# Gate attention of a decoder kernel: causal mask of the transposed scores by an elementwise minimum on VectorE

## What is computed

```python
x = _rmsnorm(hidden_states, ln1_w)
# _attention(x, Wq, Wk, Wv, Wo):
q = (x @ Wq.T).reshape(b, s, H, HD)
k = (x @ Wk.T).reshape(b, s, H, HD)
v = (x @ Wv.T).reshape(b, s, H, HD)
scores = jnp.einsum('bqhd,bkhd->bhqk', q, k) / np.sqrt(HD).astype(np.float32)
causal = jnp.tril(jnp.ones((s, s), bool))
scores = jnp.where(causal, scores, jnp.finfo(scores.dtype).min)
probs = jax.nn.softmax(scores, axis=-1)
out = jnp.einsum('bhqk,bkhd->bqhd', probs, v).reshape(b, s, d)
attn = out @ Wo.T
mod = MOD_SCALE * jnp.tanh(attn @ A)
```

## Time and profile before

| | us |
|---|---|
| median of 3 runs | 3454.83 |
| lowest, highest | 3448.98, 3464.68 |
| the profiled execution | 3458.54 |
| its span (first to last instruction) | 3456.8 |
| TensorE busy in it | 3040.2 |
| VectorE busy | 2114.3 |
| ScalarE busy | 1531.2 |

### The profile page before, as it was taken

One profiled execution on the slowest core, in us unless ns is written; L12 is line 12 of the kernel. 1 busy time (PEld: TensorE's weight loads), 2 busy tenths in 40 slices (PEclk: granted clock), 3 DMA queues, 4 the chain that ended last, 5 costly groups with the idle time before them and its releaser, 6 DMA issues. The chain is left out here.

```text
span 3456.8 us, 57813 instructions
## 1 busy us (share of the span) xinstructions
PE 3040.2 (88%) x21948; PEld 1766.5 (51%) x21948; DVE 2114.3 (61%) x2636; ACT 1531.2 (44%) x2642; POOL 938.5 (27%) x1397
## 2 busy tenths in 40 slices
PE   7999968999669968999996999599999995889997
PEld 4444323333256646888885676222222223767785
DVE  4555658999335443444444344699999992562167
ACT  3222324777533213333331333179999994321132
POOL 3444451333200001111120245423333331001154
PEclk9999986999879988999998999789999997899998
DMA  3222335555231005455443122323333323339976
GB/s 114 67 73 75 87 96 130 155 157 146 77 107 33 9 26 146 126 160 154 127 152 99 54 89 76 117 72 94 97 99 100 93 81 102 90 113 364 401 244 181
DMA packets 370294, 413.27 MB, mean 120 GB/s; under 512 B 62737, under 2 KB 246673, under 8 KB 368786
## 3 DMA queue, kind: packets, MB, share of 16 engines
q1 hardware_dynamic: 211552, 251.69, 23.6%
q10 hardware_dynamic: 135938, 100.69, 9.5%
q0 software_dynamic: 22528, 57.19, 5.5%
HBM read 299.88 MB, written 108.92 MB: 118 GB/s over the span
## 5 line engine op out<-in xcount | busy, mean ns | idle before, releaser
L394 ACT ACTIVATE c_probs<-c_st 128x512 f32<-128x512 f32 x1536 | 834.7, 597 | 214.9 <-PE c_st L320 202.6
L433 DVE TENSOR_REDUCE c_maxes<-c_s 128x2 f32<-128x1024 f32 x768 | 898.7, 1211 | 27.6 <-PE c_s L301 26.2
L337 PE MATMUL c_o<-c_probs,c_v_aug 128*32 128x256 f32 x6144 | 496.9, 395 | 46.8 <-ACT c_o_raw L404 28.9
L301 PE MATMUL c_s<-c_k_st,c_q_st 48*128 48x512 bf16 (+1 forms) x1536 | 344.8, 446 | 67.8 <-DMA c_k_st<-c_k_dram 40.1
L320 PE MATMUL c_st<-c_q_st,c_k_st 51*128 51x512 bf16 (+1 forms) x1536 | 319.6, 394 | 5.3 <-DVE c_y L459 5.1
L301 PEld LDWEIGHTS c_s<-c_k_st,c_q_st 48*128 48x128 bf16 (+1 forms) x1536 | 100.9, 128 | 401.8 <-issue 226.7
L337 PEld LDWEIGHTS c_o<-c_probs,c_v_aug 128*32 128x32 f32 x6144 | 124.4, 108 | 317.7 <-issue 214.3
L2961 DVE TENSOR_TENSOR f_w_lo<-f_w_raw,f_w_hi 128x1536 fp32r<-128x1536 f32 x64 | 116.8, 1825 | 108.7 <-ACT f_w_hi L2882 108.6
L320 PEld LDWEIGHTS c_st<-c_q_st,c_k_st 51*128 51x128 bf16 (+1 forms) x1536 | 144.0, 127 | 53.7 <-issue 23.0
L2882 ACT ACTIVATE f_w_hi<-f_w_raw 128x1536 fp32r<-128x1536 f32 x64 | 95.3, 1488 | 92.7 <-PE f_out_ps L2832 58.8
L3028 POOL CAST f_parts<-f_ctx 128x512 bf16<-128x512 f32 x16 | 12.4, 775 | 444.7 <-DMA f_ctx<-in_ctx 444.7
(11 more groups left out here) (419 smaller groups left out, 6017.7 us busy)
## 6 DMA issues: line engine op xcount, KB each, us to landing
f_w_raw<-in_f_win ACTq DMA_DIRECT2D x96, 256.0 KB, 3.1
f_w_raw<-in_f_wup ACTq DMA_DIRECT2D x96, 256.0 KB, 3.4
f_w_raw<-in_f_wdown ACTq DMA_DIRECT2D x96, 256.0 KB, 3.7
c_o_dram<-c_o_raw SPq DMA_DIRECT2D x64, 256.0 KB, 2.5
f_x<-x_dram SPq DMA_DIRECT2D x48, 256.0 KB, 4.3
c_k_dram<-f_parts ACTq DMA_DIRECT2D x96, 128.0 KB, 2.7
c_q_dram<-a_parts SPq DMA_DIRECT2D x96, 128.0 KB, 2.4
c_q_st<-c_q_dram SPq DMA_DIRECT2D x128, 96.0 KB, 2.2
```

What stands on the lines that cost most here:

```text
L301: mm = nc.tensor.matmul(s1_ps[:, i, half, :], q_st[r:r + ROWS, s, i, tt * P:(tt + 1) * P], k_st[r:r + ROWS, s, i, :], start=True, stop=True)
L337: mm = nc.tensor.matmul(o_ps[32 * h:32 * h + 32, queries], v_aug[:, (j // NG) % NBS, st, head_of(j, h), :], probs[:, (st * 4 + i * 2 + hal ...
L394: nc.scalar.activation(probs[:, e % 8, :], st_ps[:, st_bank(j, e), :], ACT.Exp).then_inc(exp_done, 1)
L433: nc.vector.tensor_reduce(maxes[:, j % 2, :].rearrange("p (h r) -> p h r", h=2)[:, :, i * KT + tt], s1_ps[:, i, :, :], AX.X, ALU.max).then ...
```

## The change

The transposed scores get their causal mask no longer by four matmuls but by a minimum with `cap_t` (f32, -1e30 where masked, 3e38 elsewhere) on VectorE, which reads PSUM and writes `probs` in SBUF (`keep`, four instructions a batch); the exponential then works in place in SBUF. The maximum is split in two f32r parts instead of three bf16 parts, in two VectorE steps instead of five, with two DMAs of f32 instead of three of bf16; `scores_t` waits for both steps. The first products of `scores_t` open the banks (start for f = 0). `scores` waits for the minima (`kept_done`), no longer for the exponentials.

```diff
         maxes = sb(f"{tag}_maxes", [P, 2, HEADS])
-        m_neg = sb(f"{tag}_m_neg", [HEADS, P])
-        m_rest = sb(f"{tag}_m_rest", [HEADS, P])
-        m_parts = sb(f"{tag}_m_parts", [HEADS, 3, P], BF16)
-        m_row = sb(f"{tag}_m_row", [P, 2, D], BF16)
+        m_parts = sb(f"{tag}_m_parts", [HEADS, 2, P], F32R)
+        m_row = sb(f"{tag}_m_row", [P, 2, D], F32R)
         probs = sb(f"{tag}_probs", [P, 2, NJ, DK, P])
...
                 def send_max(b):
-                    sp.wait_ge(m_step, 5 * (b + 1))
-                    for p in range(3):
-                        sp.dma_start(m_row[p:P:HD, b % 2, :], m_parts[:, p, :]).then_inc(m_ld, 16)
+                    sp.wait_ge(m_step, 2 * (b + 1))
+                    for p in range(2):
+                        sp.dma_start(m_row[p:P:HD, b % 2, :].bitcast(F32), m_parts[:, p, :].bitcast(F32)
+                                     ).then_inc(m_ld, 16)
...
                         if b > 0:
-                            pe.wait_ge(exp_done, 4 * (b - 1) + j + 1)
+                            pe.wait_ge(kept_done, 4 * (b - 1) + j + 1)
                         nc.tensor.matmul(sc_ps[:, j, :].rearrange("p (i s) -> p i s", i=DK), ident_bf[:, :],
...
-                    for j in range(NJ):
-                        if j == 0:
-                            pe.wait_ge(m_step, 5 * b + 1)
-                        nc.tensor.matmul(sc_ps[:, j, :].rearrange("p (i s) -> p i s", i=DK), ident_bf[:, :],
-                                         bcast(mask_t), start=True, stop=False, skip_group_check=True)
+                    pe.wait_ge(m_step, 2 * (b + 1))
                     for f in range(DK):
...
                             nc.tensor.matmul(sc_ps[:, j, f * P:(f + 1) * P], k_t[r, b // 4 % 2, f, tokens(b)],
-                                             q_t[r, b // 4 % 2, f, tokens(b)], start=False, stop=False,
+                                             q_t[r, b // 4 % 2, f, tokens(b)], start=(f == 0), stop=False,
                                              skip_group_check=True)
-                    pe.wait_ge(m_ld, 48 * (b + 1))
+                    pe.wait_ge(m_ld, 32 * (b + 1))
                     for j in range(NJ):
-                        nc.tensor.matmul(sc_ps[:, j, :], ones_bf[HD * j:HD * j + 3, :], m_row[HD * j:HD * j + 3, b % 2, :],
+                        nc.tensor.matmul(sc_ps[:, j, :], ones_r[HD * j:HD * j + 2, :], m_row[HD * j:HD * j + 2, b % 2, :],
                                          start=False, stop=True, skip_group_check=True).then_inc(st_full, 1)
...
                 def exps(b, j):
-                    act.wait_ge(st_full, b * NJ + j + 1)
-                    if b >= 2:
-                        act.wait_ge(sums_full, b - 1)
-                    nc.scalar.activation(probs[:, b % 2, j, :, :].rearrange("p f t -> p (f t)"), sc_ps[:, j, :],
-                                         ACT.Exp).then_inc(exp_done, 1)
+                    act.wait_ge(kept_done, b * NJ + j + 1)
+                    kept = probs[:, b % 2, j, :, :]
+                    nc.scalar.activation(kept, kept, ACT.Exp).then_inc(exp_done, 1)
...
                     if b > 0:
-                        dve.wait_ge(m_ld, 48 * b)
-                    nc.vector.tensor_scalar(m_neg[:, :], sc_ps[0:HEADS, 0, 0:P], -1.0, None, ALU.mult).then_inc(m_step, 1)
-                    dve.wait_ge(m_step, b * 5 + 1)
-                    nc.vector.tensor_copy(m_parts[:, 0, :], m_neg[:, :]).then_inc(m_step, 1)
-                    dve.wait_ge(m_step, b * 5 + 2)
-                    nc.vector.tensor_tensor(m_rest[:, :], m_neg[:, :], m_parts[:, 0, :], ALU.subtract).then_inc(m_step, 1)
-                    dve.wait_ge(m_step, b * 5 + 3)
-                    nc.vector.tensor_copy(m_parts[:, 1, :], m_rest[:, :]).then_inc(m_step, 1)
-                    dve.wait_ge(m_step, b * 5 + 4)
-                    nc.vector.tensor_tensor(m_parts[:, 2, :], m_rest[:, :], m_parts[:, 1, :], ALU.subtract
-                                            ).then_inc(m_step, 1)
+                        dve.wait_ge(m_ld, 32 * b)
+                    turned = sc_ps[0:HEADS, 0, 0:P]
+                    nc.vector.tensor_scalar(m_parts[:, 0, :], turned, -1.0, None, ALU.mult).then_inc(m_step, 1)
+                    dve.wait_ge(m_step, b * 2 + 1)
+                    nc.vector.scalar_tensor_tensor(out=m_parts[:, 1, :], in0=turned, scalar=-1.0, in1=m_parts[:, 0, :],
+                                                   op0=ALU.mult, op1=ALU.subtract).then_inc(m_step, 1)
+
+                def keep(b):
+                    if b == 0:
+                        dve.wait_ge(mask_ld, 16 * NMASK)
+                    if b >= 2:
+                        dve.wait_ge(sums_full, b - 1)
+                    for j in range(NJ):
+                        dve.wait_ge(st_full, b * NJ + j + 1)
+                        nc.vector.tensor_tensor(probs[:, b % 2, j, :, :],
+                                                sc_ps[:, j, :].rearrange("p (i s) -> p i s", i=DK), bcast(cap_t),
+                                                ALU.min).then_inc(kept_done, 1)
...
                 split_max(0)
+                keep(0)
...
                     normalize(b)
+                    if b + 1 < B:
+                        keep(b + 1)
                     if c + 5 < B:
...
     gate_attention(nc, "g0", x2, h_t, mod, i["f0_wq"], i["f0_wk"], i["f0_wv"], i["f0_wo"], i["f0_a"], i["f0_ln"],
-                   i["ident"], i["half"], i["ident_bf"], i["mask"], i["mask_t"])
+                   i["ident"], i["half"], i["ident_bf"], i["mask"], i["cap_t"])
     feed_forward(nc, "f0", 16, h_t, x2, x3, i["f0_win"], i["f0_wup"], i["f0_wdown"], i["half"], mod,
...
     a["mask_t"] = a["mask"].T
+    a["cap_t"] = np.where(c[:, None] > c[None, :], -1e30, 3e38).astype(np.float32)
     a["head_of"] = (c[:, None] // 32 == np.arange(4)[None, :]).astype(np.float32)
```

More of the change, by code:

```diff
@@ L705, in gate_attention @@
 def gate_attention(nc, tag, x_in, h_t_out, mod_out, wq_d, wk_d, wv_d, wo_d, a_d, ln_d, ident_d, half_d,
-                   ident_bf_d, mask_d, mask_t_d):
+                   ident_bf_d, mask_d, cap_t_d):
     R = 16
@@ L722, in gate_attention @@
         mask = sb(f"{tag}_mask", [P, P], BF16)
-        mask_t = sb(f"{tag}_mask_t", [P, P], BF16)
+        cap_t = sb(f"{tag}_cap_t", [P, P])
         wo_a = sb(f"{tag}_wo_a", [P, DK, R])
         ones = sb(f"{tag}_ones", [P, HD])
-        ones_bf = sb(f"{tag}_ones_bf", [P, P], BF16)
+        ones_r = sb(f"{tag}_ones_r", [P, P], F32R)
         x = sb(f"{tag}_x", [P, 2, D])
@@ L762, in gate_attention @@
                  "x1_done x1_hi_done x1_lo_done h_done qk_full qk_done v_full v_done s1_full max_done mT_full m_step m_ld "
-                 "st_full exp_done o_full sums_full recip_done o_normed mod_full mod_done").split()
+                 "st_full exp_done kept_done o_full sums_full recip_done o_normed mod_full mod_done").split()
         (ones_done, w_hi_done, w_lo_done, wo_a_full, wo_a_done, sumsq_done, mean_done, rstd_done, rms_done, tr_full,
          x1_done, x1_hi_done, x1_lo_done, h_done, qk_full, qk_done, v_full, v_done, s1_full, max_done, mT_full, m_step,
-         m_ld, st_full, exp_done, o_full, sums_full, recip_done, o_normed, mod_full, mod_done) = [
+         m_ld, st_full, exp_done, kept_done, o_full, sums_full, recip_done, o_normed, mod_full, mod_done) = [
              sem(f"{tag}_{n}") for n in names]
@@ L813, in _ @@
                 load(1)
-                for dst, src in ((ident_bf, ident_bf_d), (mask, mask_d), (mask_t, mask_t_d)):
+                for dst, src in ((ident_bf, ident_bf_d), (mask, mask_d), (cap_t, cap_t_d)):
                     sp.dma_start(dst[:, :], src).then_inc(mask_ld, 16)
@@ L1107, in _ @@
                 nc.vector.memset(ones[:, :], 1.0).then_inc(ones_done, 1)
-                nc.vector.memset(ones_bf[:, :], 1.0).then_inc(ones_done, 1)
+                nc.vector.memset(ones_r[:, :].bitcast(F32), 1.0).then_inc(ones_done, 1)
                 dve.wait_ge(const_ld, 16 * NCONST)
```

## The result

| | before | changed |
|---|---|---|
| median, us | 3454.83 (5 runs) | 3480.27 (5 runs) |
| lowest to highest | 3448.98 to 3464.68 | 3472.66 to 3486.98 |
| the profiled execution | 3458.54 | 3486.98 |
| the loop, from the transposition of the maxima of batch 0 to the end of the last gate's matmuls (both profiled executions) | 258.47 | 287.18 |

The ratio is 1.0059, with a 95% interval of 1.0037 to 1.0082: slower by 0.6%. The forecast was 3470.8 with a range of 3457 to 3486. Direction and the outer range held; the size came out 25 us instead of 16, 3 us outside the narrower range of 3463 to 3477 that the prediction gave as the forecast's own.

A forecast was written before the change was run, and what follows sets the result against it. Taken as bound: TensorE, with a VectorE-ScalarE chain ending alongside it without slack. Batches +11.2 us and clock +4.8 gave +16.0, so 3470.8 us against the median 3454.83; range 3457 to 3486, the forecast's own 3463 to 3477.

The forecast's parts named there:

- What bounds the kernel: Gate attention, early batches: TensorE is full, but a chain through VectorE and ScalarE ends at the same moment.
- The statement that the sum turned on: Early batches: the chain split, reciprocal, mean, norm, exponentials has no slack; values start 0.10 us after the last exponential.
- The minima and the split: VectorE's tail: four minima add 2.44 us, the shorter split saves 0.77, so mean and what follows move +1.67.
- the range given: TensorE's four f32r ones matmuls: 0.33 us side by side to 1.0 one after the other; 0.33 to 0.5 taken.
- the cover that the text called just enough: Minima's wait for st_full: seen at T+4.7, VectorE free at T+4.85, T being the start of the maxima's transposition.
- The sum by batch: Gate loop, unchanged clock: batches 1-7 +11.7 us, 8-10 -2.3, 11-15 +3.3, batch 0 -1.5; together +11.2.
- The clock: TensorE's granted clock halves after some new holes: three drops expected at 1.6 us each, +4.8; least certain term.
- the prediction's own sign: Changed trace: the forecast counts as wrong if the clock drops number none or six.
- the seven new holes: TensorE, batches 1 to 7: five holes of 3 us ahead of values, two of 5 ahead of the projection.
- Rival (a): TensorE's clock falls after each of seven holes: 17.5 us instead of 4.8, +28.7, total 3483.5; chance 0.17.
- (b): VectorE's minima delay nobody and the mask's 0.96 us is gained in 15 batches: -15.9, total 3438.9; chance 0.04.
- (c): TensorE's f32r ones matmuls run one after the other: +2.1 us, total 3472.9; chance 0.78 together with the forecast.

The follow-up runs named there:

- delay_alone_b: Kernel before plus four unread 128x512 VectorE instructions between product and mean, masks, exponentials and split as before; 3483.83 us, ratio 1.0068.
- fill_both_b: fill_holes plus 11 unread matmuls ahead of the transposition of the maxima of batches 12 to 15; 3463.22 us, ratio 1.0017 to the kernel before.
- fill_holes: Changed kernel plus unread matmuls in TensorE's holes ahead of values (batches 1, 2, 4-6, 11-15) and projection (3, 7); 3473.25 us, ratio 1.0040 to before.
- split_alone: Kernel before with only the two-part f32r maximum: two VectorE steps, two DMAs, f32r ones matmuls; 3457.03 us, ratio 0.9996.

## Why the prediction was right, and where it was off

**What bounds the kernel.** Right. The statement that the sum turned on, that the chain over VectorE's mean and ScalarE's queue ends with TensorE and has no slack, is shown by delay_alone_b, which delays nothing but that chain: the mean and the values both move by 2.41 us, four steps of VectorE 0.60 apart.

**The minima and the split.** 2.44 - 0.77 = +1.67 was forecast, +1.85 measured (T+9.71 to T+11.56). The minima came 0.60 apart, the split saved 0.81. Two small terms were missing. The ones matmuls in f32r take 0.42 for the four instead of 0.33 (1122.79 to 1123.21), inside the range given, but the first of them is seen by VectorE 0.58 after its start, not 0.4: the minima wait 0.13 for st_full, the cover that the text called just enough. And the exponentials out of SBUF last 2.17 for four instead of 2.04: in these batches 613 ns each against 593, but their starts are 0.52 apart instead of 0.48, some 37 ns more (1.55 against 1.44 over three intervals). The estimate by the Trainium skill ("VectorE: DVE Perf Modes", section on the TRN2 errata) of 43 ns for each was nearer to this than the 0.02 that was read off the duration of another operation; what counts here is the distance of the starts. Seven batches by 0.13 are 0.9 us, where the estimate by the Trainium skill came to 1.2.

**The sum by batch, at full clock** (fill_both_b against before): batches 1 to 7 +12.3 (forecast +11.7), 8 to 10 -2.65 (-2.3), 11 to 15 +2.7 (+3.3), batch 0 -0.6 (-1.5). Together +11.8 (+11.2). In batch 0 the ones matmuls started at T+3.85 instead of T+5.08, 1.23 earlier, but values only 0.6 earlier (T+9.54 instead of T+10.12). In both kernels the clock was at half until about T+9, so of the projection, which began earlier, more fell into the slow stretch; the prediction had priced the gain as if it were carried through.

**The clock.** This is the term that was mis-sized: +4.8 was forecast, 16.9 measured (18.5 of drops in the changed kernel less the 1.55 of the one drop before), and filling the holes removed it. By the prediction's own sign (wrong if the drops number none or six) it failed: ten batches dropped. Two faults. Of the seven new holes, five were followed by a drop, not three: 1.7, 2.5, 1.6, 1.7 and 1.3 us, 8.7 in all. And the holes of batches 11 to 15 were not counted at all: their chain was priced at +0.66, but the step overlooked that the two short holes ahead of values (0.49 and 0.64 of TensorE in the kernel before) become 0.54 and 2.05, before the one of 2.63. All five batches dropped, 1.3 to 2.8 us each (in the last two the clock was low twice), 9.6 together; in the kernel before it was one of five, besides a low stretch at the end, around the hole of 4.19 us ahead of the last gate, which both kernels have and the prediction's count of drops left out. That the holes stand so close is not shown to be the reason: with the one of 2.05 filled (fill_holes) the clock still fell in 12 to 15.

Rival (a), the clock falling behind every new hole, was the nearest to the mark with its 3483.5. That its 17.5 us agree with the 16.9 measured is luck: its seven holes cost 8.7, and the rest came from batches that it did not count. The outer range held because its upper end, 3486, made room for this rival; the forecast's own ended at 3477.

**Rivals.** (b), that nobody is delayed, is out by delay_alone_b. (c), f32r matmuls one after the other, is out: 0.42 for four.

## What to carry to other kernels

Before work is put on an engine with room on average, look at what stands behind it in that engine's queue and who waits for that; in delay_alone_b 2.4 us went through three in-order queues to an engine that needed none of the new results, and in the changed kernel two lines in another order took 17 of the loop's 29 us away. Price a new hole on TensorE twice, once for its length and once for the work behind it at half clock, and count every hole that grows, also where the chain is hardly longer. A mask, a split or an order that is best in one batch need not be so in the next: the version that chose by batch beat both kernels.

## What was not expected of the hardware

- In the changed kernel the granted clock of TensorE fell to half (1.2 GHz) around three of five holes of 2.7 us, around both of 4.7 and 5.4, and in all of batches 11 to 15, whose larger holes are 2.05 to 2.64 long, but for 4.18 ahead of the last gate. In batch 11 it fell at T+7.3, inside the hole of 2.05. Matmuls without use in these holes held it at 1.00 in batches 1 to 14 and made the loop 18.5 us shorter.
- The length of the hole alone didn't decide it: in batch 3 the clock stayed full behind 2.85 us in the kernel before and fell behind 2.01 us in split_alone.
- ScalarE's exponentials of 128x512 start 0.52 apart out of SBUF and 0.48 out of PSUM, where nothing holds them.
- Four f32r matmuls of 2 rows on four row groups, 512 columns, take 0.42 us, the bf16 ones with 3 rows 0.33.
